# The taps of a state-space convolution: tables of powers and quarter-width products in place of 16 sine tables

## The chip, the cores and the metric

One core of one Trainium2 chip runs the program. The metric is the device time of one execution in microseconds (us), lower is better. The core's engines run side by side and wait for one another only through semaphores: TensorE (PE, with its weight loads as PEld), VectorE (DVE), ScalarE (ACT), GpSimd (POOL) and SyncE (SP), which issues the DMAs.

## The reference

The input x has 4 sequences of 1024 positions and 256 channels. Three residual steps are applied; the inputs of each are layer-normalized.

```
x = x + 0.5 * ffn(layernorm(x))
x = x + s4(layernorm(x))
x = x + 0.5 * ffn(layernorm(x))

ffn(x): h = silu(x w1' * w1_s) * (x w2' * w2_s)       # 256 -> 1024, ternary weights
        h = gelu(h h1' * h1_s); h = gelu(h h2' * h2_s)  # 1024 -> 1024, twice
        return h w3' * w3_s                             # 1024 -> 256
s4(x):  dt = exp(log_dt); A = -exp(log_A_real) + 1j * A_imag; dtA = A * dt   # 32 states per channel
        C = (C_real + 1j * C_imag) * (exp(dtA) - 1) / A
        K[d, t] = 2 * Re(sum_n C[d, n] * exp(dtA[d, n] * t))   # t = 0 .. 1023, the taps
        y = causal convolution of x with K along the positions (by FFT)
        return gelu(y) @ W' + b
```

The change touches only how the taps K are computed: 256 channels x 32 states x 1024 positions of complex exponentials, summed over the states.

## The kernel before

The 4096 rows are cut into tiles of 512. `ALL` = 16 tiles T = 0 to 15 go through the feed-forward net: T = 0 to 7 for the first ffn, T = 8 to 15 for the second. A tile has 24 steps k. Steps 0 to 7 are layer one: TensorE makes two products, VectorE gates them (`gate`), ScalarE and VectorE split the result into a high and a low part, since every product with activations is done for both (`hid_a_hi` and `hid_a_lo`, `hid_b_hi` and `hid_b_lo`). Steps 8 to 15 are the second layer and 16 to 23 the third, one `hidden` each: 16 matmuls 128x512 on TensorE, Gelu on ScalarE (L546), then `split` on VectorE (a CAST, L1167, and a subtraction, L1169). TensorE needs ScalarE's result of step k - 4 before it begins step k, because four PSUM banks go round, and ScalarE needs the split of step k - 3, because `act_o` has three slots. At k = 16 the inputs are the splits of steps 8 to 15, at `layer_three` (L1306) those of 16 to 23: there TensorE depends on the newest splits at once.

All order is written out by hand. Each engine runs through the same T and k in its own block of code, and the other work hangs on certain (T, k):

- `prepare` (VectorE, ScalarE, in T = 0 and 1) makes dt, decay and the angles from the parameters. A table of 8 block factors per channel and state is made by GpSimd (`angles8`, `powers8`, in T = 0 and 1).
- The taps. State and real or imaginary part lie on the 128 partitions, a pair of channels at each of 128 indices i, and a block of 128 positions on a table's columns. In 16 pieces c of `CH` = 8 indices each, placed by `turned_at` at every other k of T = 1 to 3, GpSimd makes the phases (`phase`, L473) and seven doublings of the decay (`doubles`, L482), VectorE reduces the phases to one turn (`turn_steps`, L844 to L848), ScalarE takes the sine (`sines`, L588), VectorE multiplies by the decay (`table_step`, L853), and TensorE multiplies (`tap_step`, L1313): 8 float32 matmuls with the 128-column table as weights and 16 columns (`kp`) that stream.
- The sums end in PSUM banks 4 to 7, are copied to `kt` in T = 3, and from T = 4 on are mirrored (`mirror_taps`), folded and transformed. T = 4 to 12 also carry the spectral convolution, one batch in two tiles.
- The layer norms (`norm_begin` L811 to L819, `norm_end` L824) sit on VectorE at the steps of `norm1_at` and `norm2_at`.

What `prepare` and `turn_steps` do on VectorE stands in its queue between two splits, so it delays every split behind it.

## Time and profile before

| | us |
|---|---|
| median of 3 runs | 1529.27 |
| lowest and highest | 1526.87, 1532.13 |
| the profiled execution | 1530.53 |
| its span, first to last instruction | 1528.7 |
| TensorE busy in the span | 1476.5 |
| VectorE, ScalarE, GpSimd busy | 1046.0, 521.9, 209.5 |
| mean granted TensorE clock | 0.988 of full |

A tile's time is read between two ends of its last product's scaling on VectorE (L1221). The span is the profiler's; the execution's own time is 1.8 us longer. In rows of the trace a number in square brackets is the idle time of that engine just before the instruction, with what ended it.

### The profile page before, as it was taken

How to read it: one execution, taken by the hardware profiler on the slowest of the kernel's cores; microseconds unless marked ns; L12 is line 12 of the kernel's file. 1: busy time of each engine (PE TensorE's matmuls, PEld its weight loads, DVE VectorE, ACT ScalarE, POOL GpSimd, SP SyncE). 2: the span in 40 equal slices, each digit the busy share in tenths (PEclk: the TensorE clock that was granted, in tenths of full speed). 3: DMA queues.
4: the chain of work that ended last, by engine and by line, in shares of the span. 5: the costliest groups of instructions: out<-in, count | busy, mean ns of one | idle time of the engine just before them, and what ended most of it. 6: DMA issues, size and time to landing. Idle time of an engine off the chain costs nothing.

```text
span 1528.7 us, 17472 instructions
## 1 busy us (share of the span) xinstructions
PE 1476.5 (97%) x6910; PEld 1192.3 (78%) x6910; DVE 1046.0 (68%) x1731; ACT 521.9 (34%) x743; POOL 209.5 (14%) x205
## 2 busy tenths in 40 slices
PE   7988979989999999999999999999999999999998
PEld 3767867777787778878778787787888878888886
DVE  7787576967857878785787848777587865343432
ACT  4623235445542332422323232232322324142321
POOL 0033553744600000001000010000000010000000
PEclk9999989999999999999999999999999999999999
DMA  8000000000001322103121031121221212000000
GB/s 347 15 0 28 28 14 15 28 15 14 28 15 39 116 91 83 43 25 124 42 83 56 13 123 56 55 70 39 68 69 42 69 38 69 0 15 28 29 1 15
DMA packets 52116, 78.27 MB, mean 51 GB/s; under 512 B 2752, under 2 KB 44736, under 8 KB 50624
## 3 DMA queue, kind: packets, MB, share of 16 engines
q1 hardware_dynamic: 52032, 77.12, 14.9%
q8 instruction: 56, 0.92, 0.2%
q14 instruction: 28, 0.23, 0.0%
HBM read 56.14 MB, written 20.97 MB: 50 GB/s over the span
## 4 chain that ended last, share of the span: by engine, by line
PE 81%; DVE 8%; issue 7%; ACT 3%; POOL 1%; DMA 0%; POOLq 0%; DVEq 0%; ACTq 0%
PE ps L1244 64%; PE ps L1306 7%; PE ps L1343 3%; PE ps L1396 2%; PE ps L1313 2%; DVE hid_a_lo L1169 1%; ACT L588 1%; DVE table L853 1%; ACT ph L588 1%; DVE hid_a_hi L1167 1%; DVE table L846 1%; PE ps L1235 1%; PE ps L1337 1%; PE ps L1338 1%; PE ps L1386 0%
## 5 line engine op out<-in xcount | busy, mean ns | idle before, releaser
L546 ACT ACTIVATE act_o<-ps,scales 128x512 f32<-128x512 f32 x384 | 263.8, 688 | 936.1 <-PE ps L1244 930.0
L1244 PE MATMUL ps<-hid_b_hi,h 128*128 128x512 f32 x1024 | 406.9, 397 | 4.9 <-DVE hid_b_lo L1169 4.7
L1244 PE MATMUL ps<-hid_b_lo,h 128*128 128x512 f32 x1024 | 403.3, 394 | 0.0
L1244 PE MATMUL ps<-hid_a_hi,h 128*128 128x512 f32 x992 | 395.8, 399 | 1.2 <-DVE hid_a_lo L1160 0.8
L1244 PE MATMUL ps<-hid_a_lo,h 128*128 128x512 f32 x992 | 390.8, 394 | 0.0
L1244 PEld LDWEIGHTS ps<-hid_b_hi,h 128*128 128x128 f32 x1024 | 193.6, 189 | 50.2 <-DVE hid_b_lo L1169 7.0
L1244 PEld LDWEIGHTS ps<-hid_b_lo,h 128*128 128x128 f32 x1024 | 193.5, 189 | 43.3 <-issue 1.2
L1244 PEld LDWEIGHTS ps<-hid_a_hi,h 128*128 128x128 f32 x992 | 187.6, 189 | 48.7 <-DVE hid_a_lo L1160 3.7
L1244 PEld LDWEIGHTS ps<-hid_a_lo,h 128*128 128x128 f32 x992 | 187.7, 189 | 42.1 <-issue 2.2
L1244 PE MATMUL ps<-hid_b_hi,w 128*128 128x512 f32 x480 | 190.0, 396 | 2.4 <-DVE gz L1221 2.1
L1244 PE MATMUL ps<-hid_b_lo,w 128*128 128x512 f32 x480 | 188.7, 393 | 0.0
L421 POOL TENSOR_TENSOR rstd<-vare,expo 128x4 f32<-128x4 f32 x24 | 27.9, 1163 | 920.1 <-DVE vare L819 920.1
L1167 DVE CAST hid_a_hi<-act_o 128x512 fp32r<-128x512 f32 x128 | 61.8, 483 | 129.3 <-ACT act_o L546 128.8
L1167 DVE CAST hid_b_hi<-act_o 128x512 fp32r<-128x512 f32 x128 | 55.4, 433 | 137.9 <-ACT act_o L546 137.6
L1306 PE MATMUL ps<-w,hid_a_hi 128*128 128x256 f32 x512 | 127.6, 293 | 15.2 <-DVE hid_a_lo L1169 9.6
L1155 DVE SCALAR_TENSOR_TENSOR gz<-ps,scales,act_o 128x512 f32<-128x512 f32 x128 | 96.0, 750 | 65.7 <-ACT act_o L546 64.0
L1306 PE MATMUL ps<-w,hid_a_lo 128*128 128x256 f32 x512 | 123.6, 285 | 0.0
L1244 PEld LDWEIGHTS ps<-hid_b_hi,w 128*128 128x128 f32 x480 | 90.1, 188 | 33.4 <-DVE gz L1155 8.1
L1306 PEld LDWEIGHTS ps<-w,hid_a_hi 128*128 128x128 f32 x512 | 100.9, 197 | 18.8 <-DVE hid_a_lo L1169 10.5
L1244 PEld LDWEIGHTS ps<-hid_b_lo,w 128*128 128x128 f32 x480 | 90.3, 188 | 16.1 <-issue 0.2
L1169 DVE TENSOR_TENSOR hid_a_lo<-act_o,hid_a_hi 128x512 fp32r<-128x512 f32 x128 | 99.3, 776 | 4.4
L1306 PEld LDWEIGHTS ps<-w,hid_a_lo 128*128 128x128 f32 x512 | 100.9, 197 | 1.1 <-issue 1.0
(228 smaller groups left out, 1597.6 us busy)
## 6 DMA issues: line engine op xcount, KB each, us to landing
ks<-k_d SPq DMA_DIRECT2D x32, 512.0 KB, 3.8
raws<-in_weights SPq DMA_DIRECT2D x11, 1024.0 KB, 15.6
gz<-in_x SPq DMA_DIRECT2D x8, 512.0 KB, 3.8
xin<-in_x SPq DMA_DIRECT2D x8, 512.0 KB, 3.9
x_d<-xin SPq DMA_DIRECT2D x8, 512.0 KB, 2.9
z_d<-xin SPq DMA_DIRECT2D x8, 512.0 KB, 2.9
k_d<-ks SPq DMA_DIRECT2D x8, 512.0 KB, 2.6
zb<-z_d SPq DMA_DIRECT2D x8, 512.0 KB, 5.4
```

The lines of the kernel that those rows point to most:

```text
L421: G.tensor_tensor(rstd[:, :], vare[:, :], expo[:, :], ALU.pow).then_inc(s_rstd, 1)
L546: A(act_o[:, k % ACT_SLOTS], bank(source), func, scale=scale).then_inc(s_act, 1)
L588: A(ph[:, c % 2], ph[:, c % 2], ACT.Sin, scale=TWO_PI_DOWN).then_inc(s_sin, 1)
L846: V.tensor_scalar(r_, r_, MAGIC, col(C_PH), ALU.subtract, ALU.subtract).then_inc(s_rnd, 1)
L1155: V.scalar_tensor_tensor(gated[:, m % 2], bank(2 * (m % 2) + 1), scales[:, 1, m:m + 1], act_o[:, m % ACT_SLOTS], ALU.mult, ALU.mult).then_ ...
L1167: V.tensor_copy(hi[:, k % KH], source).then_inc(s_hi, 1)
L1169: V.tensor_tensor(lo[:, k % KH], source, hi[:, k % KH].bitcast(F32), ALU.subtract).then_inc(s_split, 1)
L1244: last = MM(o, weight[:, k, cols].bitcast(dt), part[:, k].bitcast(dt), start=(k == 0 and i == 0), stop=(k == n - 1 and i == len(act_) - 1))
L1306: last = MM(o, part[:, k, j * P:(j + 1) * P].bitcast(dt), w3[:, k].bitcast(dt), start=(k == 0 and i == 0), stop=(k == KH - 1 and i == 1))
L1313: last = MM(ps[:, 4 + i // 32, (i % 32) * 2 * A8:(i % 32 + 1) * 2 * A8], table[:, c % 2, i % CH, :], kp[:, i, 0:2 * A8], start=True, stop= ...
L1343: last = MM(bank(o), tables[:, table_], flat(x), start=True, stop=True)
L1396: last = MM(o, ga[:, k, u * P:(u + 1) * P], wt[:, k], start=(k == 0), stop=(k == KD - 1))
```

## The change

Before, a tap's position is t = 128 a + q, with 8 blocks a and a table of 128 positions q that needs a sine for each entry. Now it is t = 32 a + q with 32 positions q and 32 blocks a, both tables are products of small tables of powers, and no sine is left in the loop over pieces. `prepare` now makes ten seeds: the complex exponential at 1, 2, 4, ... 512 positions (`ea` the sizes, `sn` and `cs` the sine and cosine), with two sine instructions of 1280 columns in T = 1 (`sines`) and the reciprocals in parts of 128 columns. From the seeds VectorE and ScalarE multiply up two small tables per channel, `v` (8 powers) and `u` (4 powers), each once for the positions and once for the blocks; 4 x 8 = 32 (`SPAN`) entries come from each pair of tables. For each of 8 pieces of 16 indices, `make_factors` on VectorE forms the 32-column tables `tab` and `gr` (six operations 128x512), ScalarE writes `gr` masked by channel half into the 64 columns of `gm`, and `multiply_taps` on TensorE does 16 float32 matmuls with 32 weight columns and 64 streaming columns, each with its result in one quarter of the 128 partitions of PSUM. `MADE`, `MASKED` and `MULTIPLIED` say at which (T, k) each stands. GpSimd's work on the taps goes away but for four memsets. Since the sums now lie by quarters, ScalarE copies them out at T = 3, k = 17 into `wb`, and SyncE turns them by a DMA to memory and four back into `zb` (`turn_taps`). Several norms move by one to three steps, and the rest of the coefficient arithmetic moves from T = 0 into T = 1. Nothing from T = 4, k = 8 on is altered.

```diff
+SEEDS = 10
 EXPS = SEEDS // 2
-KPAR = 2 * A8 + 1 + DBL
+NV, NU = 8, 4
+PIECE = 16
+PIECES = P // PIECE
+SPAN = NU * NV
...
-def turned_at(T):
-    return {1: {20: 0, 22: 1}, 2: {8 + 2 * i: 2 + i for i in range(8)},
-            3: {8 + 2 * i: 10 + i for i in range(6)}}.get(T, {})
+MADE = {(2, 17): 0, (2, 19): 1, (2, 21): 2, (3, 8): 3, (3, 9): 4, (3, 10): 5, (3, 11): 6, (3, 14): 7}
+MASKED = {(2, 18): 0, (2, 20): 1, (2, 22): 2, (3, 9): 3, (3, 10): 4, (3, 11): 5, (3, 12): 6, (3, 15): 7}
+MULTIPLIED = {(2, 20): 0, (2, 22): 1, (3, 8): 2, (3, 11): 3, (3, 12): 4, (3, 13): 5, (3, 14): 6, (3, 17): 7}
...
+            def turn_taps():
+                sp.wait_ge(s_kev, 1)
+                sp.dma_start(t_d, wb[:, :, :].rearrange("p u d -> p (u d)")).then_inc(s_kd, 16)
+                sp.wait_ge(s_kd, 16)
+                by_block = t_d.rearrange("(g t) (b f) -> b t g f", g=4, b=4)
+                for b in range(4):
+                    home = zb[32 * b:32 * b + 32].rearrange("t u d -> t (u d)").rearrange("t (g f) -> t g f", g=4)
+                    sp.dma_start(home, by_block[b]).then_inc(s_kt, 16)
...
-            def phase(c):
-                if c >= 2:
-                    pool.wait_ge(s_table, c - 1)
-                G.tensor_tensor(ph[:, c % 2], kp[:, c * CH:(c + 1) * CH, 2 * A8:2 * A8 + 1].to_broadcast([P, CH, P]),
-                                taps[:, :].unsqueeze(1).to_broadcast([P, CH, P]), ALU.mult).then_inc(s_phase, 1)
-            def doubles(c):
-                if c:
-                    pool.wait_ge(s_table, c)
-                for k in range(DBL):
-                    n = 1 << k
-                    seed = kp[:, c * CH:(c + 1) * CH, 2 * A8 + 1 + k:2 * A8 + 2 + k].to_broadcast([P, CH, n])
-                    G.tensor_tensor(dec[:, :, n:2 * n], dec[:, :, 0:n], seed, ALU.mult).then_inc(s_dbl, 1)
-                    pool.wait_ge(s_dbl, c * DBL + k + 1)
...
+            pool.wait_ge(s_seed, 1)
+            for powers, value in ((vre, 1.0), (vim, 0.0), (ure, 1.0), (uim, 0.0)):
+                last = G.memset(powers[:, :, :, 0:1], value)
+            last.then_inc(s_units, 1)
...
-            def sines8(h):
-                act.wait_ge(s_arg8, h + 1)
-                for i in (0, 1):
-                    A(tap8[:, i], tap8[:, i], ACT.Sin, scale=TWO_PI_DOWN).then_inc(s_sin8, 1)
+            def sines():
+                act.wait_ge(s_arg, 3)
+                A(sn[:, :], cs[:, :], ACT.Sin, scale=TWO_PI_DOWN).then_inc(s_fun, 1)
+                act.wait_ge(s_fun, 4)
+                A(cs[:, :], cs[:, :], ACT.Sin, scale=PI_DOWN).then_inc(s_fun, 1)
+            def copy_seeds(homes, v, k):
+                for home, seeds in zip(homes, (cs, sn)):
+                    A(home[:, :, :, v], seeds[:, k:k + EXPS + 1:EXPS], ACT.Copy).then_inc(s_copied, 1)
...
+                    act.wait_ge(s_arg, 4)
+                    A(et[:, :], er[:, :], ACT.Tanh, scale=0.5)
                     A(tmp[:, 5], tmp[:, 9], ACT.Tanh, scale=0.5).then_inc(s_fun, 1)
-                    for i in (2, 3, 4):
-                        A(tmp[:, 4 + i], tmp[:, i], ACT.Sin, scale=TWO_PI_DOWN).then_inc(s_fun, 1)
-                if T == 1 and k == 2:
-                    sines8(0)
-                if T == 1 and k == 15:
-                    sines8(1)
...
+                    copy_seeds((vre, vim), 4, 2)
+                    copy_seeds((ure, uim), 1, 3)
+                    copy_seeds((ure, uim), 2, 4)
+                if T == 2 and k == 10:
+                    act.wait_ge(s_tabled, 1)
+                    act.wait_ge(s_units, 1)
+                    act.wait_ge(s_copied, 10)
+                    A(xt[:, 0], uim[:, 0], ACT.Copy, scale=small[:, C_NRE:C_NRE + 1])
+                    A(xt[:, 1], ure[:, 0], ACT.Copy, scale=small[:, C_RE:C_RE + 1]).then_inc(s_turned, 1)
+                if (T, k) in MASKED:
+                    n = MASKED[T, k]
+                    act.wait_ge(s_factor, n + 1)
+                    if n:
+                        act.wait_ge(s_tap, n)
+                    for j in range(2):
+                        last = A(gm[:, :, j], gr[:, :, :], ACT.Copy, scale=small[:, C_H + j:C_H + j + 1])
+                    last.then_inc(s_masked, 1)
...
-                if T == 3 and k == PER_U - 2:
-                    act.wait_ge(s_tap, SUBS)
-                    for i in (0, 2):
-                        last = A(zb[:, 2 * i:2 * i + 4].rearrange("p u d -> p (u d)"), bank(4 + i, 2), ACT.Copy)
-                    last.then_inc(s_kt, 1)
+                if T == 3 and k == 17:
+                    act.wait_ge(s_tap, PIECES)
+                    sums = ps[:, 4:8, :].rearrange("p n c -> p (n c)").rearrange("p (f a b) -> p b f a", a=A8, b=4)
+                    homes = wb[:, :, :].rearrange("p u d -> p (u d)").rearrange("p (b f a) -> p b f a", b=4, a=A8)
+                    for b in range(4):
+                        last = A(homes[:, b], sums[:, b], ACT.Copy)
+                    last.then_inc(s_kev, 1)
                 if T == 4:
...
                 if T == 0 and k == 11:
                     dve.wait_ge(s_fun, 1)
+                    step(V.tensor_scalar(er[:, 0:2], et[:, 0:2], -1.0, 1.0, ALU.mult, ALU.add))
+                    step(V.reciprocal(er[:, 0:2], er[:, 0:2]))
+                if T == 0 and k == 12:
                     step(exp_finish(tmp[:, 0:2], 2))
-                    step(V.scalar_tensor_tensor(decay, ar, -1.0, dt_, ALU.mult, ALU.mult))
+                    V.scalar_tensor_tensor(decay, ar, -1.0, dt_, ALU.mult, ALU.mult).then_inc(s_arg, 1)
                     step(V.tensor_tensor(tmp[:, 10], ai, dt_, ALU.mult))
-                    V.tensor_scalar(turns, tmp[:, 10], INV_TWO_PI, None, ALU.mult)
-                    for i in range(EXPS):
-                        last = V.tensor_scalar(ea[:, i], decay, float(4 ** i), None, ALU.mult)
+                    step(V.tensor_scalar(cs[:, 0], tmp[:, 10], INV_TWO_PI, None, ALU.mult))
+                if T == 0 and k == 15:
+                    for first, n in ((1, 1), (2, 2), (4, 1), (5, 5)):
+                        step(V.tensor_scalar(cs[:, first:first + n], cs[:, 0:n], float(2 ** first), None, ALU.mult))
+                    step(V.tensor_scalar(sn[:, :], cs[:, :], MAGIC, -MAGIC, ALU.add, ALU.add))
+                if T == 0 and k == 16:
+                    V.tensor_tensor(cs[:, :], cs[:, :], sn[:, :], ALU.subtract).then_inc(s_arg, 1)
+                    dve.wait_ge(s_fun, 2)
+                    exp_reduce(ea[:, 0:EXPS], EXPS, 0)
+                if T == 0 and k == 17:
+                    exp_reduce(ea[:, 0:EXPS], EXPS, 1)
+                if T == 0 and k == 18:
+                    exp_reduce(ea[:, 0:EXPS], EXPS, 2).then_inc(s_arg, 1)
+                if T == 0 and k == 19:
+                    V.tensor_tensor(a2, ar, ar, ALU.mult)
+                    step(V.tensor_tensor(q1, ai, ai, ALU.mult))
+                    step(V.tensor_tensor(q2, a2, q1, ALU.add))
+                    step(V.reciprocal(a2, q2))
+                if T == 0 and k == 20:
+                    dve.wait_ge(s_fun, 3)
+                    step(V.tensor_scalar(er[:, :], et[:, :], -1.0, 1.0, ALU.mult, ALU.add))
+                if T == 0 and k in (20, 21):
+                    for i in range(EXPS)[0 if k == 20 else 2:2 if k == 20 else EXPS]:
+                        last = V.reciprocal(er[:, i], er[:, i])
                     step(last)
...
+                if T == 1 and k == 8:
                     step(exp_finish(ea[:, 0:EXPS], EXPS))
                     step(V.tensor_tensor(ea[:, EXPS:], ea[:, 0:EXPS], ea[:, 0:EXPS], ALU.mult))
...
+                if T == 1 and k == 9:
+                    dve.wait_ge(s_fun, 5)
+                    step(V.scalar_tensor_tensor(cs[:, :], cs[:, :], -2.0, cs[:, :], ALU.mult, ALU.mult))
+                    step(V.tensor_copy(versed, cs[:, 0]))
+                    step(V.tensor_scalar(cs[:, :], cs[:, :], 1.0, None, ALU.add))
...
+                if T == 1 and k in (17, 18):
+                    seeds = (sn, cs)[k - 17][:, :].rearrange("p (i h) q -> p i h q", h=2)
+                    sizes = ea[:, :].rearrange("p (h i) q -> p i h q", h=2)
+                    last = V.tensor_tensor(seeds, seeds, sizes, ALU.mult)
+                    if k == 17:
+                        step(last)
+                    else:
+                        last.then_inc(s_seed, 1)
...
+                if (T, k) in ((1, 21), (2, 8)):
+                    part = 2 - T
+                    if T == 1:
+                        dve.wait_ge(s_copied, 4)
+                    x = vre[:, :, :, 1:4], vim[:, :, :, 1:4]
+                    y = [h.unsqueeze(3).to_broadcast([P, 2, P, 3]) for h in power(2)]
+                    last = product((vre[:, :, :, 5:8], vim[:, :, :, 5:8]), x, y, ct[:, :, :, :], T - 1)
+                    if T == 1:
+                        step(last)
+                    else:
+                        last.then_inc(s_tabled, 1)
...
+            def make_factors(n):
+                q = slice(n * PIECE, (n + 1) * PIECE)
+                wide = [P, PIECE, NU, NV]
+                for s_, out_ in ((0, tab[:, n % 2]), (1, gr[:, :, :])):
+                    if s_ == 0 and n >= 2:
+                        dve.wait_ge(s_tap, n - 1)
+                    if s_ == 1 and n:
+                        dve.wait_ge(s_masked, n)
+                    out_ = out_.rearrange("p q (u v) -> p q u v", v=NV)
+                    extra = pt[:, :, :].rearrange("p q (u v) -> p q u v", v=NV)
+                    for to, u, v in ((out_, (uim, ure)[s_], vre), (extra, (ure, uim)[s_], vim)):
+                        last = V.tensor_tensor(to, u[:, s_, q].unsqueeze(3).to_broadcast(wide),
+                                                v[:, s_, q].unsqueeze(2).to_broadcast(wide), ALU.mult)
+                    step(last)
+                    last = V.tensor_tensor(out_, out_, extra, ALU.add)
+                    if s_:
+                        last.then_inc(s_factor, 1)
                     else:
                         step(last)
...
-            def turn_steps(c):
-                p_, r_ = ph[:, c % 2], table[:, c % 2]
-                dve.wait_ge(s_phase, c + 1)
-                if c >= 2:
-                    dve.wait_ge(s_tap, c - 1)
-                V.tensor_scalar(r_, p_, col(C_PH), MAGIC, ALU.add, ALU.add).then_inc(s_rnd, 1)
-                dve.wait_ge(s_rnd, 2 * c + 1)
-                V.tensor_scalar(r_, r_, MAGIC, col(C_PH), ALU.subtract, ALU.subtract).then_inc(s_rnd, 1)
-                dve.wait_ge(s_rnd, 2 * c + 2)
-                V.tensor_tensor(p_, p_, r_, ALU.subtract).then_inc(s_red, 1)
-            def table_step(c):
-                dve.wait_ge(s_sin, c + 1)
-                dve.wait_ge(s_dbl, (c + 1) * DBL)
-                V.tensor_tensor(table[:, c % 2], ph[:, c % 2], dec[:, :, :], ALU.mult).then_inc(s_table, 1)
...
-            def tap_step(c):
-                pe.wait_ge(s_table, c + 1)
-                for i in range(c * CH, (c + 1) * CH):
-                    last = MM(ps[:, 4 + i // 32, (i % 32) * 2 * A8:(i % 32 + 1) * 2 * A8], table[:, c % 2, i % CH, :],
-                              kp[:, i, 0:2 * A8], start=True, stop=True)
+            def multiply_taps(n):
+                pe.wait_ge(s_masked, n + 1)
+                for i in range(PIECE):
+                    r, g = divmod(n * PIECE + i, 4)
+                    width = 2 * SPAN
+                    at = r % 8 * width
+                    last = MM(ps[SPAN * g:SPAN * (g + 1), 4 + r // 8, at:at + width], tab[:, n % 2, i],
+                              gm[:, i].rearrange("p j a -> p (j a)"), start=True, stop=True)
                 last.then_inc(s_tap, 1)
...
-                pe.wait_ge(s_kt, 1)
+                pe.wait_ge(s_kt, 16 * 4)
```

TensorE in the third layer of a tile, T = 3. Before, a tap step stands in front of every other `hidden` (33 rows apart, eight in T = 2 and eight in T = 3):

```order
1229 L1244 MATMUL ps<-hid_a_hi,h_51 128x512
1230 L1244 MATMUL ps<-hid_a_lo,h_51 128x512
1231 L1313 MATMUL ps<-kp,table 128x16 x8
1232 L1244 MATMUL ps<-hid_a_hi,h_51 128x512
1233 L1244 MATMUL ps<-hid_a_lo,h_51 128x512
```

and now (two of these pieces in T = 2, six in T = 3, four of them at successive k):

```order
1206 L1249 MATMUL ps<-hid_a_hi,h_51 128x512
1207 L1249 MATMUL ps<-hid_a_lo,h_51 128x512
1208 L1321 MATMUL ps<-gm,tab 32x64 x16
1209 L1249 MATMUL ps<-hid_a_hi,h_51 128x512
1210 L1249 MATMUL ps<-hid_a_lo,h_51 128x512
```

The stop has twice as many matmuls, a quarter of the weight columns and four times the streaming columns, and there are half as many stops.

VectorE in T = 0 at k = 11 and 12, before; `ek`, `er`, `et` are the exponential's parts, `ea` the sizes:

```order
50 L726 TENSOR_SCALAR er<-et 128x256
51 L727 RECIPROCAL er<-er 128x256
52 L728 SCALAR_TENSOR_TENSOR er<-et,er 128x256
53 L729 TENSOR_TENSOR tmp<-er,ek 128x256
54 L749 SCALAR_TENSOR_TENSOR tmp<-tmp 128x128
55 L750 TENSOR_TENSOR tmp<-par,tmp 128x128
56 L751 TENSOR_SCALAR kp<-tmp 128x128
57 L753 TENSOR_SCALAR ea<-tmp 128x128 x5
58 L1167 CAST hid_b_hi<-act_o 128x512
59 L1169 TENSOR_TENSOR hid_b_lo<-act_o,hid_b_hi 128x512
60 L716 TENSOR_SCALAR ek<-ea 128x640
```

and now:

```order
50 L711 TENSOR_SCALAR er<-et 128x256
51 L712 RECIPROCAL er<-er 128x256
52 L1173 CAST hid_b_hi<-act_o 128x512
53 L1175 TENSOR_TENSOR hid_b_lo<-act_o,hid_b_hi 128x512
54 L675 SCALAR_TENSOR_TENSOR er<-et,er 128x256
55 L676 TENSOR_TENSOR tmp<-er,ek 128x256
56 L715 SCALAR_TENSOR_TENSOR tmp<-tmp 128x128
57 L716 TENSOR_TENSOR tmp<-par,tmp 128x128
58 L717 TENSOR_SCALAR cs<-tmp 128x128
59 L1173 CAST hid_b_hi<-act_o 128x512
```

The work of k = 11 is spread over two steps, and the seven operations on 640 columns that began at row 60 follow only behind k = 15.

## Rows read from the trace of the kernel before

In the windows a row is the stretch and its length in us, the busy us (and instructions) of PE, PEld, DVE, ACT and POOL, the granted TensorE clock as a share of full speed, the DMA share and GB/s.

**Rows 1.** Windows, one row for each of T = 0 to 3, then T = 14.

```profile
0.00:127.36 127.36, 107.05 (x409) 75.64 (x410) 96.74 (x167) 51.07 (x59) 16.29 (x19) 0.96 0.28 109
127.36:223.52 96.16, 87.09 (x394) 71.65 (x393) 64.57 (x94) 32.73 (x46) 54.53 (x47) 0.93 0.07 22
223.52:333.78 110.26, 101.60 (x522) 84.17 (x521) 86.16 (x111) 53.69 (x61) 59.15 (x66) 0.97 0.06 20
333.78:438.90 105.12, 99.80 (x519) 82.28 (x518) 73.76 (x105) 51.88 (x60) 42.67 (x49) 0.98 0.07 21
...
1359.55:1441.33 81.78, 81.78 (x394) 67.77 (x393) 35.61 (x66) 24.66 (x37) 1.01 (x1) 1.00 0.06 20
```

**Rows 2.** Waits of TensorE, 0 to 534.2 us: total, times, longest.

```profile
PE ps L1313 <- DVE table L853: 10.5, 14, 0.8
PE ps L1306 <- DVE hid_a_lo L1169: 9.6, 4, 3.5
...
PE ps L1306 <- ACT act_o L546: 4.9, 2, 4.3
PE ps L1244 <- DVE hid_b_lo L1169: 4.7, 3, 2.3
```

**Rows 3.** Waits of TensorE in T = 0 alone, 0 to 127.36 us.

```profile
PE ps L1306 <- DVE hid_a_lo L1169: 3.3, 2, 3.0
```

**Rows 4.** Timeline of TensorE around one tap step in T = 2.

```profile
245.58 0.39 PE L1244 MATMUL ps<-hid_a_hi,h 128*128 128x512 f32 x1
245.81 0.40 PE L1244 MATMUL ps<-hid_a_lo,h 128*128 128x512 f32 x1
246.95 1.96 PE L1313 MATMUL ps<-kp,table 128*128 128x16 f32 x16 [0.74 <-DVE table L853]
248.76 0.48 PE L1244 MATMUL ps<-hid_a_hi,h 128*128 128x512 f32 x1
```

**Rows 5.** Windows: two stretches of low granted clock, T = 2 and T = 1.

```profile
249.65:253.06 3.41, 3.41 (x10) 2.65 (x9) 2.51 (x4) 0.00 (x0) 3.02 (x6) 0.51 0.00 0
...
205.20:218.85 13.65, 8.35 (x37) 8.05 (x38) 9.61 (x9) 4.12 (x5) 8.74 (x10) 0.50 0.00 0
```

**Rows 6.** Timeline of T = 0, VectorE and TensorE, 66 to 84 us.

```profile
66.73 1.75 DVE L727 RECIPROCAL er<-er 128x256 f32<-128x256 f32 x1
...
71.03 0.43 DVE L1167 CAST hid_b_hi<-act_o 128x512 fp32r<-128x512 f32 x1
...
76.33 0.42 DVE L1167 CAST hid_b_hi<-act_o 128x512 fp32r<-128x512 f32 x1
...
82.40 0.69 DVE L1169 TENSOR_TENSOR hid_b_lo<-act_o,hid_b_hi 128x512 fp32r<-128x512 f32 x1
...
83.15 0.79 PE L1244 MATMUL ps<-hid_b_hi,h 128*128 128x512 f32 x1 [1.89 <-DVE hid_b_lo L1169]
```

**Rows 7.** Timeline of the end of T = 1.

```profile
196.60 3.98 POOL L473 TENSOR_TENSOR ph<-kp,taps 128x1024 f32<-128x1024 f32 x2
196.66 2.14 DVE L1167 CAST hid_a_hi<-act_o 128x512 fp32r<-128x512 f32 x1
...
203.87 1.06 ACT L588 ACTIVATE ph<-ph 128x1024 f32<-128x1024 f32 x1 [3.70 <-DVE ph L848]
...
206.98 0.58 PE L1306 MATMUL ps<-w,hid_a_hi 128*128 128x256 f32 x1 [4.29 <-ACT act_o L546]
```

**Rows 8.** Groups by line: operations nearest to the new ones; last numbers: busy, mean ns.

```profile
L1313 PE MATMUL ps<-kp,table 128*128 128x16 f32 x256 | 31.3, 264 | 10.5 <-DVE table L853 10.5
...
L588 ACT ACT_TABLE_LOAD x16 | 20.5, 1283 | 0.3
...
L874 DVE TENSOR_TENSOR wb<-ps,zb 128x256 f32<-128x256 f32 x4 | 2.4, 594 | 0.0
```

**Rows 9.** The one-column matmul's line: weight loads, ns min/median/max.

```profile
L1448 PEld LDWEIGHTS ps<-single x2: 79/80/81, 54.9 to 54.9; 128*1 128x1 f32 x2
```

**Rows 10.** Timeline: eight float32 passes of 512 columns in T = 10.

```profile
1037.35 3.60 PE L1343 MATMUL ps<-fb,tables 128*128 128x512 f32 x8
```

314 lines of the change are left out of this document (121 added, 193 removed).

## The prediction

> **What bounds the kernel now.** I first split the span by tiles. A tile without taps or spectral work, T = 14, takes 81.78 us, and TensorE is busy for all of it. T = 1, 2 and 3 take 96.16, 110.26 and 105.12 us, and T = 0 takes 127.36 [rows 1]. So TensorE sets the end everywhere, and T = 1 to 3 hold 14.4 + 28.5 + 23.3 = 66.2 us above the plain tile. Next the waits of TensorE in this stretch: 9.6 and 4.9 us stand before layer three and 4.7 us before the third layer at k = 16, together 19.2 us in few, long waits, and 10.5 us stand before tap steps in 14 short ones [rows 2]. Then one tap step in the timeline: the last `hidden` matmul starts at 245.81, the next could start 0.23 us later, and starts at 248.76. The step costs 2.72 us: 0.74 us of waiting for the table, 16 passes at 0.112 us (1.96 us less the tail of the last), and small rests [rows 4]. Last the clock: 249.65 to 253.06 is granted 0.5, the lower level of 1.2 GHz against 2.4, just after such a step; in T = 1, 205.20 to 218.85 is low, around two long waits before layer three [rows 5]. The granted clock times the length gives 5.1 us lost in T = 0, and 6.7, 3.3 and 2.1 in T = 1 to 3 [rows 1]; in T = 1 TensorE stood still for 5.3 of the 13.65 low us [rows 5], so only 4.2 us count there, 14.7 in all.
>
> These three causes close the account: T = 1 to 3 have 11.1 us of the long waits (19.2 less 4.7 and 3.3 in T = 0 [rows 2, 3]), 16 x 2.72 = 43.5 us of tap steps and 9.6 us of clock, 64.2 of the 66.2 us.
>
> **The change, part by part.**
>
> *T = 0, VectorE's queue.* At k = 11 and 12 `prepare` holds it from the reciprocal at 66.73 to the CAST at 71.03, and again from that split's end to 76.33: with 1.1 us for the split in between, 4.6 us (a scalar operation of 0.3 is ahead of the reciprocal) and 4.2 us. Behind them the norm and three splits queue up, the last ends at 83.09, and TensorE stops for it, 1.89 us at that place [rows 6]. Now k = 11 is 0.3 + 1.8 us and k = 12 about 1.7 us. 8.8 - 3.8 = 5.0 us less lie before split 15, more than the 4.7 us of waits, which go. The seven operations on 640 columns come after k = 15 in three parts, each with its split under 3.7 us, and a `hidden` is 16 x 0.23 = 3.67 us [rows 4]: TensorE covers them. Behind k = 22 and 23, where the coefficient arithmetic stood, nothing is left, so T = 0's 3.3 us before layer three [rows 3] go too.
>
> *T = 1, ScalarE and VectorE.* TensorE's 4.29 us wait goes back to ScalarE, which stood 3.70 us for VectorE's reduced phases, and VectorE was late since a CAST that takes 0.43 us elsewhere took 2.14 us beside GpSimd's phases [rows 6, 7]. Phases and sines are gone. In their place the sines of 1280 columns, 2 x 1.3 + 1.28 us for the table [rows 7, 8], stand on ScalarE ahead of step 8. That makes split 8 about 4 us late. VectorE's new work in k = 8 to 14 is 2.6, 2.7, 2.4 us, by about 1.05 us for 1000 elements of a product, then two norms of 3.4 (76.33 to 83.09 is one norm and three splits of 1.1 [rows 6]); with seven splits of 1.1 us that is 22.2 us against 25.7 us of TensorE, so the 4 us shrink to about half a microsecond where split 15 is needed. This is the thinnest cover: if it fails, up to 4 us of wait return. From k = 15 to 21 the parts are 1.4 to 3.0 us, and ScalarE's ten seed copies are 0.4 us each, all inside a step.
>
> *Layer boundaries together:* 19.2 us go, and I leave 1.0 us for the new ones: -18.2.
>
> *The pieces on VectorE and ScalarE.* A piece is six operations of two inputs on 128x512, as the 0.69 us of L1169 [rows 6], 4.2 us, with a split 5.3 us. Four stand at successive k = 8 to 11 of T = 3. TensorE's step there is 3.67 us and a piece of matmuls, t; with t of 1.7 us or more VectorE keeps up. The masks are two ScalarE operations of 512 columns, some 0.6 us each by 1.06 for 1024 [rows 7]; each is placed a step or more ahead of its matmuls, in T = 2 with a margin of about nothing for the first. The piece at k = 14 ends close to the need at k = 16. What is late next there is split 15, 0.2 to 0.5 us, in the 1.0 us above. VectorE's table work was five operations on 1024 columns for each of 16 steps.
>
> *The matmuls.* 8 stops of 32 passes replace 16 of 16. Lower bound of a pass: by streaming alone. Eight passes of 512 columns take 3.60 us, less a tail 0.43 us each, 0.84 ns a column [rows 10], so 64 columns take 0.054 us. Upper bound of a pipelined pass: as before, 0.112 us [rows 4], which a 16-column stream cannot set, so the weight load or the issue does. A load of one column takes 0.080 us [rows 9], a load of T = 14, nearly all of 128 columns, 0.172 us (67.77 us by 393 [rows 1]); 32 columns lie nearer the first. I take 0.083, the middle, since the issue rate is unknown. t = 32 x 0.083 + 0.15 to enter = 2.8 us, 8 t = 22.4 instead of 43.5: -21.1. With the bounds t is 1.8 or 3.7 and the term -29 or -14.
>
> The Trainium skill (TensorE: Matmul & The Clock Gate, LDWEIGHTS) has the load go by its columns alone, which would let streaming set the pass: an estimate of 7 us less than my sum. By that section the one-column load must be the shorter one, and the trace agrees, 0.080 against 0.172 us [rows 1, 9]; no row has 32 columns.
>
> *Clock.* 14.7 us are lost now. The long waits that stood beside three of the low stretches go; eight stops instead of sixteen remain. Of the sixteen one in T = 2 had a low stretch behind it [rows 5], 1.7 us, and the 2.1 us of T = 3, which has no long wait, are about one more [rows 1, 2]. I keep 4 us: -10.7.
>
> *Tap layout.* ScalarE copies out at k = 17 (four of 512 columns, 2.4 us) and the round trip is five DMAs. TensorE asks at T = 4, k = 0, six steps, transposes and layer three later, over 29 us. Hidden; with no cover it would cost its own time, some 10 us. The mirror matmuls and folds keep count and size, 0; if the new stride doubled the streaming of the mirror's eight passes of 256 columns, 0.215 us each by 0.84 ns a column [rows 10], it would be +1.7.
>
> Sum: -18.2 - 21.1 - 10.7 = -50.0. The profiled execution took 1530.53 us, 1.3 over the median of the three runs, so against that median **1529.3 - 50 = 1479 us**.
>
> **The rivals.**
>
> *Same pace, more low clock (20 of 100).* A pass stays at 0.112 us: t = 3.7, +7 us. A stop is then longer than the old one, and each may be followed by a low stretch as after 248.76 [rows 4, 5]: 8 x 1.7 = 13.6 instead of 4, +10. 1486 to 1496. For it: the 16-column pass shows that something else than streaming sets the pace. Against: the stream is four times longer, and a load has a quarter of the columns.
>
> *Quarters at the same time (10 of 100).* Four successive matmuls use four different quarters of the output. If they overlap, a stop is streaming by four, 0.5 us, 8 t = 4 to 5 us instead of 22. Then VectorE sets the pace at four successive pieces, 5.3 us against 4.2, and gives 4 us back: 1465. No row here has two matmuls at once. The Trainium skill says it can be so (TensorEngine Tiling (Array Packing), Key Properties: tiles work independently, weight loads and matmuls in parallel).
>
> *VectorE becomes the bound (10 of 100).* The one product here that reads with large steps, L874, takes 0.594 us for 256 elements [rows 8], where a plain product of 512 takes 0.69 [rows 6]. If repeated and stepped operands make a product of 512 elements 1.05 us, a piece is 6.3 and a step 7.4 us against 6.5: four pieces lose 4 us, k = 14 loses 2 to 3, T = 1's tables the rest of their cover: 1487. Against: the innermost operand of each product is dense or repeats.
>
> *The other side: drained quarters (5 of 100).* If each pass must wait until the one before has left the array, it costs a load and a full matmul, 0.08 to 0.19 + 0.264 us [rows 8, 9], t = 11 to 14.6, 8 t = 88 to 117: 1545 to 1573. It decides from t = 2.8 + 50/8 = 9.0 us, 0.28 us a pass. Milder, a drain only where a stop begins and ends costs 0.26 us each by the same row, 4 us in all, inside the range. The Trainium skill (TensorEngine Tiling (Array Packing), Key Properties) has such a rule: a change of tiling mode drains TensorE, a change of the tile alone does not.
>
> **How the numbers follow.** 55 of 100 for the sum as worked out, with 1468 to 1489 as its own range (t from 1.8 to 3.2, clock 0 to 8 us, waits 0 to 5). The rivals have 20, 10, 10 and 5. The range takes in all but the drained quarters and the outer ends: 1464 to 1500. A difference of 0.3%, 4.6 us, is about what a measurement of this kernel can tell from none. Faster: 93, within: 2, slower: 5.
>
> **What would show it.** Right: T = 0 near 114 us, T = 1 near 83, T = 2 near 88, T = 3 near 100; no wait over 1 us before k = 16 or layer three; starts of the new passes 0.055 to 0.112 us apart; no GpSimd beside VectorE in T = 1 to 3. Wrong: passes over 0.2 us apart; ScalarE late at step 8 of T = 1 and a wait at its k = 16; TensorE waiting for ScalarE's masks in T = 3; low clock behind most of the eight stops; the mirror matmuls of T = 4 waiting for a DMA.

## The result, and the profile after

| | before | after |
|---|---|---|
| median, us | 1528.90 (4 runs) | 1461.55 (4 runs) |
| lowest and highest | 1526.87, 1532.13 | 1461.34, 1463.29 |
| the profiled execution, its span | 1530.53, 1528.7 | 1463.29, 1461.0 |
| TensorE busy | 1476.5 | 1437.8 |
| VectorE, ScalarE, GpSimd busy | 1046.0, 521.9, 209.5 | 986.4, 476.6, 48.1 |
| mean granted clock | 0.988 | 0.998 |

The ratio is 0.956, 95% interval 0.9542 to 0.9579: 67 us less, where 50 were forecast. 1461.55 lies 2.5 us below the range. The same windows as in [rows 1]:

```profile
0.00:115.01 115.01, 102.36 (x409) 72.35 (x410) 82.06 (x131) 48.71 (x59) 2.47 (x8) 1.00 0.31 120
115.01:196.78 81.77, 81.77 (x394) 67.76 (x393) 63.37 (x127) 32.21 (x49) 4.42 (x6) 1.00 0.08 26
196.78:280.46 83.68, 83.61 (x458) 68.75 (x457) 57.99 (x109) 29.93 (x45) 2.01 (x2) 1.00 0.08 26
280.46:369.49 89.03, 87.33 (x583) 70.11 (x582) 57.73 (x110) 32.97 (x51) 2.12 (x2) 1.00 0.16 48
```

T = 0 to 3 are 12.4, 14.4, 26.6 and 16.1 us shorter, 69.4 in all. T = 1 is now a plain tile: TensorE is busy for all of it, while VectorE has 63 us of work beside it. The granted clock is full in all four. The one new loss is behind them, at the start of T = 5, where the clock is low for 3.41 us (1.7 us lost):

```profile
465.80:469.21 3.41, 3.41 (x10) 2.63 (x9) 1.33 (x3) 0.76 (x2) 0.00 (x0) 0.50 0.84 263
```

The waits of TensorE over the first 534 us, where [rows 2] had 29.7 us at four places. The 2.1 us stand at the start of T = 5, which in the kernel before lay just behind this window:

```profile
PE ps L1249 <- DVE gz L1226: 2.1, 1, 2.1
PE ps L1321 <- ACT gm L534: 1.6, 3, 0.5
...
PE ps L1249 <- DVE hid_b_lo L1175: 0.3, 1, 0.3
```

L1249 is `hidden`, L1321 the taps' matmul, L534 the mask, L1175 the split's subtraction. Nothing before layer three is left in T = 0 to 3. One stop for the taps in the timeline, answering [rows 4]:

```profile
332.82 0.40 PE L1249 MATMUL ps<-hid_b_lo,h 128*128 128x512 f32 x1
333.15 0.65 PE L1321 MATMUL ps<-gm,tab 128*32 128x64 f32 x32
333.73 0.51 PE L1249 MATMUL ps<-hid_b_hi,h 128*128 128x512 f32 x1
```

From the `hidden` matmul before to the one behind it are 0.91 us, 0.23 of which are that matmul's own: the stop costs 0.68 us, for 32 passes. The price of each of the eight is 0.67 to 0.82 us with no wait or one under 0.1 us, and 1.26 to 1.28 where the mask is late, 7.4 us in all. The sixteen of before, priced in the same way, cost 41.6 us and not the 43.5 of the prediction: 2.72 us holds for the fourteen with a wait, but the first stop of T = 2 and the first of T = 3 had none and cost 1.70 us each:

```profile
236.69 0.39 PE L1244 MATMUL ps<-hid_b_lo,w 128*128 128x512 f32 x1
236.92 1.85 PE L1313 MATMUL ps<-kp,table 128*128 128x16 f32 x16
238.62 0.48 PE L1244 MATMUL ps<-hid_a_hi,h 128*128 128x512 f32 x1
```

The 32 starts within the first new stop, in ns after one another:

```
7 7 6 60 7 7 6 36 7 6 7 36 7 6 ...   last start 435 ns after the first
```

Four passes start within 20 ns, and then there is a gap. The profile does not name the quarters; that the four go into four different ones is inferred from the run one_quarter below, where passes into the same quarter never start less than 55 ns apart. The groups by line:

```profile
L534 ACT ACTIVATE gm<-gr,small 128x512 f32<-128x512 f32 x16 | 10.7, 716 | 15.3 <-DVE gr L832 15.3
...
L829 DVE TENSOR_TENSOR tab<-uim,vre 128x512 f32<-128x512 f32 x8 | 5.5, 685 | 0.0
...
L1321 PE MATMUL ps<-gm,tab 128*32 128x64 f32 x256 | 5.2, 222 | 1.6 <-ACT gm L534 1.6
L1321 PEld LDWEIGHTS ps<-gm,tab 128*32 128x32 f32 x256 | 3.9, 109 | 4.9 <-ACT gm L534 4.1 <-issue 0.7
...
L1329 PE MATMUL ps<-zb,flip 128*128 128x256 f32 x8 | 3.6, 608 | 0.0
```

The matmul's row has 222 ns for one from start to end and the load's 109, so a pass does not finish in 7 ns: several are under way at once (the profile models a matmul's end, but the starts and the price of the stop do not hang on it). In both rows x256 counts passes, two for each float32 matmul.

### The profile page after: what moved, and what is told of

It is laid out like the page before. It is cut to its first block, busy times and chain, and to the rows that moved or that the text cites. A ratio compares the mean times of both kernels' runs of the same rounds, so it can differ in the third digit from the quotient of the medians.

```text
span 1461.0 us, 17259 instructions
## 1 busy us (share of the span) xinstructions
PE 1437.8 (98%) x6910; PEld 1159.7 (79%) x6910; DVE 986.4 (68%) x1729; ACT 476.6 (33%) x721; POOL 48.1 (3%) x42
## 3 DMA queue, kind: packets, MB, share of 16 engines
q1 hardware_dynamic: 52464, 79.15, 16.1%
## 4 chain that ended last, share of the span: by engine, by line
PE 92%; DVE 6%; ACT 1%; issue 1%; DMA 0%; POOL 0%; DVEq 0%; ACTq 0%; POOLq 0%
PE ps L1249 76%; PE ps L1311 8%; PE ps L1344 3%; PE ps L1397 2%; PE ps L1240 1%; DVE hid_b_lo L1175 1%; PE ps L1338 1%; PE ps L1339 1%; DVE pt L829 1%; PE ps L1387 0%; DVE hid_b_hi L1173 0%; ACT act_o L476 0%; DVE low L1140 0%; DVE tab L832 0%; DVE gr L832 0%
## 5 line engine op out<-in xcount | busy, mean ns | idle before, releaser
L1249 PE MATMUL ps<-hid_b_hi,h 128*128 128x512 f32 x1024 | 404.4, 395 | 0.5 <-DVE hid_b_lo L1175 0.3
L1249 PE MATMUL ps<-hid_b_lo,h 128*128 128x512 f32 x1024 | 401.6, 392 | 0.0
L1249 PE MATMUL ps<-hid_a_hi,h 128*128 128x512 f32 x992 | 393.1, 396 | 0.2
L1249 PE MATMUL ps<-hid_a_lo,h 128*128 128x512 f32 x992 | 388.7, 392 | 0.0
L1249 PEld LDWEIGHTS ps<-hid_b_hi,h 128*128 128x128 f32 x1024 | 192.5, 188 | 44.8 <-DVE hid_b_lo L1175 1.4
L1249 PEld LDWEIGHTS ps<-hid_b_lo,h 128*128 128x128 f32 x1024 | 192.5, 188 | 43.1 <-issue 1.2
L1249 PEld LDWEIGHTS ps<-hid_a_hi,h 128*128 128x128 f32 x992 | 186.3, 188 | 47.5 <-DVE hid_a_lo L1166 2.8
L1249 PEld LDWEIGHTS ps<-hid_a_lo,h 128*128 128x128 f32 x992 | 186.4, 188 | 41.4 <-issue 2.2
L1249 PE MATMUL ps<-hid_b_hi,w 128*128 128x512 f32 x480 | 190.3, 396 | 2.1 <-DVE gz L1226 2.1
L1249 PE MATMUL ps<-hid_b_lo,w 128*128 128x512 f32 x480 | 189.6, 395 | 0.0
L1173 DVE CAST hid_a_hi<-act_o 128x512 fp32r<-128x512 f32 x128 | 56.7, 443 | 135.4 <-ACT act_o L476 134.7
L1311 PE MATMUL ps<-w,hid_a_hi 128*128 128x256 f32 x512 | 123.0, 286 | 0.8 <-ACT act_o L476 0.8
L1311 PE MATMUL ps<-w,hid_a_lo 128*128 128x256 f32 x512 | 119.8, 279 | 0.0
L1249 PEld LDWEIGHTS ps<-hid_b_hi,w 128*128 128x128 f32 x480 | 90.6, 189 | 32.5 <-DVE gz L1161 7.8
L1249 PEld LDWEIGHTS ps<-hid_b_lo,w 128*128 128x128 f32 x480 | 90.9, 189 | 16.3 <-issue 0.2
L1311 PEld LDWEIGHTS ps<-w,hid_a_hi 128*128 128x128 f32 x512 | 96.6, 189 | 3.3 <-ACT act_o L476 1.2
L1311 PEld LDWEIGHTS ps<-w,hid_a_lo 128*128 128x128 f32 x512 | 96.6, 189 | 1.1 <-issue 1.0
L1175 DVE TENSOR_TENSOR hid_a_lo<-act_o,hid_a_hi 128x512 fp32r<-128x512 f32 x128 | 88.6, 693 | 4.4
L1175 DVE TENSOR_TENSOR hid_b_lo<-act_o,hid_b_hi 128x512 fp32r<-128x512 f32 x128 | 88.6, 692 | 4.4
```

The costliest lines, as they stand in the source:

```text
L1173: V.tensor_copy(hi[:, k % KH], source).then_inc(s_hi, 1)
L1175: V.tensor_tensor(lo[:, k % KH], source, hi[:, k % KH].bitcast(F32), ALU.subtract).then_inc(s_split, 1)
L1249: last = MM(o, weight[:, k, cols].bitcast(dt), part[:, k].bitcast(dt), start=(k == 0 and i == 0), stop=(k == n - 1 and i == len(act_) - 1))
L1311: last = MM(o, part[:, k, j * P:(j + 1) * P].bitcast(dt), w3[:, k].bitcast(dt), start=(k == 0 and i == 0), stop=(k == KH - 1 and i == 1))
```

## The experiments

**One quarter.** All 16 products of a piece go to the same quarter of PSUM's partitions (the sums lie elsewhere, so the taps are not those of the reference; the work is the same).

```diff
-                    last = MM(ps[SPAN * g:SPAN * (g + 1), 4 + r // 8, at:at + width], tab[:, n % 2, i],
-                              gm[:, i].rearrange("p j a -> p (j a)"), start=True, stop=True)
+                    g, slot = n // 2, n % 2 * PIECE + i
+                    last = MM(ps[SPAN * g:SPAN * (g + 1), 4 + slot // 8, slot % 8 * width:(slot % 8 + 1) * width],
+                              tab[:, n % 2, i], gm[:, i].rearrange("p j a -> p (j a)"), start=True, stop=True)
```

> All 16 products of a piece go to one quarter of the partitions (pieces 0 and 1 to the first, 2 and 3 to the second, and so on), same weight loads, same streams, same count; the sums land in the wrong places, so the taps are wrong. Theory A: neighbouring products overlap because they use different quarters. Then the 32 passes of a piece follow one another at 0.054 (streaming) to 0.112 us (the old pass), a piece costs 1.9 to 3.7 us in place of 0.67 to 0.82, eight of them +9 to +24 us: 1470 to 1486 us. Rival B: a pass of 32 weight columns and 64 streaming columns is short by itself, whatever the quarter: starts stay 7 to 60 ns apart and the time stays at 1461.5.

**Two quarters** in turn within a piece (the taps again misplaced).

```diff
+                    g, slot = n // 4 * 2 + i % 2, n % 4 * (PIECE // 2) + i // 2
```

> The products of a piece alternate between two quarters; the sums land in the wrong places. Theory A: two passes at a time, a piece costs about half of the one-quarter piece, 1.0 to 1.9 us. Rival B: no change, 0.7 us a piece.

**Grouped.** The changed kernel's own 16 products, with those of the same quarter behind one another.

```diff
-                for i in range(PIECE):
+                for i in [4 * b + a for a in range(4) for b in range(PIECE // 4)]:
```

> The same 16 products with the same places as in the changed kernel, in another order: four for the first quarter, then four for the second, and so on. Theory A with overlap only between neighbours of different quarters: overlap at 3 of 15 borders alone, a piece costs 1.5 to 3 us. Theory A with a queue for each quarter that is filled ahead: as in the changed kernel, 0.7 us. Rival B: 0.7 us.

**Full width.** Four positions' tables together as 128 weight columns, all quarters at once, 64 columns streaming (the taps are not those of the reference).

```diff
-                    last = MM(ps[SPAN * g:SPAN * (g + 1), 4 + r // 8, at:at + width], tab[:, n % 2, i],
+                    four = tab[:, n % 2, i // 4 * 4:i // 4 * 4 + 4].rearrange("p q a -> p (q a)")
+                    last = MM(ps[:, 4 + r // 8, at:at + width], four,
```

> Each product has 128 weight columns (the tables of four indices side by side) and the same 64 streaming columns, and fills all 128 partitions; three quarters of each result are overwritten or useless, so the taps are wrong. If 128 weight columns set the pass as before, starts are 0.112 us apart, a piece costs 3.7 us and the eight cost +24 us less the 1.6 us of mask waits: 1483 to 1486. If streaming sets it, 0.054 us, 1.9 us a piece, about 1470. If the count of passes alone matters (rival B), 1461.5. Also: whether stops of 3.7 us are followed by a low granted clock, which would add up to 1.7 us each (the prediction's second rival, up to 1499).

**Narrow stream.** As full width, but 16 columns stream.

```diff
-                              gm[:, i].rearrange("p j a -> p (j a)"), start=True, stop=True)
+                              gm[:, i, 0, 0:16], start=True, stop=True)
```

> The changed kernel, but each of the 16 products of a piece takes four positions' tables as weights (all 128 columns, all 128 partitions of the result) and streams only 16 columns, as the tap products of the kernel before did; the taps are then not those of the reference. If the load of 128 weight columns sets the pace, a pass is 0.112 us apart as in the kernel before and as with 64 streaming columns, a piece costs 3.4 to 3.6 us, and the whole is 1484 to 1487 us. If streaming counted beside the load, 16 columns would go faster than the 64 of full_width: under 0.10 us a pass and below 1482. On the clock: if stops with a thin stream bring low clock by themselves, low stretches follow the pieces of T = 2 and 3 here; if they came from the waits that stood before them, none does.

**Quarter narrow and four narrow.** One quarter, and the changed kernel, with 16 streaming columns.

> one_quarter with 16 streaming columns in place of 64 (the taps are not those of the reference; the first piece also has four products 128x512 ahead of its own, so that no sum is unset, some 3.5 us once). It settles what the 0.056 us of a pass in one quarter is. If streaming sets it, 0.84 ns by 16 columns would be 0.013 us, and a pass falls to whatever the load of 32 weight columns needs, 0.03 us by a quarter of 0.112: first to last start of a piece about 0.9 us and a piece 1.2. Rival: the load and the entry of the next pass in the same quarter set it, then passes stay 0.056 us apart and a piece costs 2.0 us. On the clock: if a stream of 16 columns is what brings the clock down, a low stretch may follow here too, though the stop is shorter than in narrow_stream.

> The changed kernel with 16 streaming columns in place of 64, the four quarters in turn as in the changed kernel (the same parts of the computation are altered as in quarter_narrow). Four neighbours start 7 ns apart and a group takes 56 ns. If streaming sets the group, 16 columns make it 30 ns or less and a piece falls from 0.70 to 0.5 us; if four loads of 32 columns, 14 ns each, set it, a piece stays at 0.67 to 0.70 us. The time is then 1461 to 1465 us (3.5 us of it for the first piece's extra products).

**Twice.** The changed kernel with the loop over a piece's products run two times.

```diff
-                for i in range(PIECE):
+                for i in list(range(PIECE)) * 2:
```

> The changed kernel with each piece's 16 products issued twice, the second time with the same operands into the same places, so 64 passes in a stop. It separates what a pass costs from what it costs to enter and leave a stop. If the passes cost what their starts show (32 in 0.435 us), a piece of 0.70 to 0.82 us becomes 1.15 to 1.3, eight give +3.0 to 3.8 us: 1464.5 to 1467. Rival: the starts are only issue and the array works longer behind them, or most of a piece is entry: then the second half costs 0.7 us or more each (+5.6, 1469), or under 0.2 us (+1.5, 1463 to 1465).

What the eight kernels gave beside the changed one, measured as above (steady distance of starts within a piece; a piece without a wait; all eight pieces, with waits, and without the extra products of the two that have them):

| kernel | weight columns, streaming | distance of starts, ns | first to last, us | a piece, us | eight, us | span, us |
|---|---|---|---|---|---|---|
| full_width | 128, 64 | 112 | 3.41 | 3.49 | 28.5 | 1482.2 |
| narrow_stream | 128, 16 | 112 | 3.38 | 3.49 | 30.0 | 1490.9 |
| one_quarter | 32, 64 | 56 | 1.76 | 1.99 | 16.2 | 1466.6 |
| quarter_narrow | 32, 16 | 32 | 1.00 | 1.21 | 10.1 | 1465.5 |
| grouped | 32, 64 | 56, and 6, 50, 30, 26, 30, 26, 30 across borders | 1.18 | 1.42 | 11.5 | 1462.4 |
| two_quarters | 32, 64 | 7 and 49: 56 a pair | 0.87 | 1.11 | 9.5 | 1461.9 |
| changed kernel | 32, 64 | 7, 7, 7, 36: 56 a group | 0.44 | 0.68 | 7.4 | 1461.0 |
| four_narrow | 32, 16 | 7, 7, 7, 12: 32 a group | 0.26 | 0.47 | 6.3 | 1462.6 |
| twice | 32, 64, 64 passes | as the changed kernel | 0.88 | 1.12 | 9.6 | 1463.1 |

Two ran four times: one_quarter 1470.99 (ratio to before 0.9608, 0.9575 to 0.9642), full_width 1485.24 (0.9698, 0.9665 to 0.9731). The other six ran once each (two_quarters 1464.06, grouped 1464.64, narrow_stream 1493.01, twice 1465.34, quarter_narrow 1467.59, four_narrow 1464.76), so what follows rests on their traces, not on these times. Four of the stops as timelines show them, one_quarter, full_width, narrow_stream and four_narrow:

```profile
340.00 1.98 PE L1322 MATMUL ps<-gm,tab 128*32 128x64 f32 x32
```

```profile
328.27 0.39 PE L1249 MATMUL ps<-hid_a_lo,h 128*128 128x512 f32 x1
328.50 3.68 PE L1322 MATMUL ps<-gm,tab 128*128 128x64 f32 x32
331.99 0.48 PE L1249 MATMUL ps<-hid_a_hi,h 128*128 128x512 f32 x1
```

```profile
326.03 3.64 PE L1322 MATMUL ps<-gm,tab 128*128 128x16 f32 x32
```

```profile
336.06 0.45 PE L1324 MATMUL ps<-gm,tab 128*32 128x16 f32 x32
```

A piece in one quarter costs 2.0 us and in four 0.68, with the same operands and counts. That shows that the quarters overlap; a pace set by the issue of instructions would have been the same in both. The prices of a piece in quarter_narrow, four_narrow and twice came as the first theory of each had them; their spans hold the first piece's extra products (the first two) and no low clock at T = 5 (twice). All eight pieces of twice cost 2.2 us more than the changed kernel's, not the 3.0 to 3.8 expected, because at three of them the added passes only fill the time in which TensorE waited for a mask. narrow_stream has the pace expected and 6 us more than the time expected, for which see the clock below.

What follows, step by step. *The load:* with 128 weight columns a pass is 0.112 us for 16 and for 64 streaming columns, so the load set it in the kernel before too. With 32 it is 0.056 us in one quarter; 16 streaming columns bring it to 0.032. So at 64 columns streaming sets the pass (0.84 ns by 64 is 0.054, my lower bound's argument), and the floor below it is 0.032, little over a quarter of 0.112. That this floor is the load is argued from that proportion. *The quarters:* two in turn take the 56 ns for a pair, four for a group of four. The time is that of one quarter's stream, shared. The products' order matters: grouped has the changed kernel's own products and needs 1.42 us in place of 0.68. Neither theory had that number. Overlap of the two neighbours at each of the three borders alone would save about 3 x 0.05 us of one_quarter's 1.76 from first to last start, but grouped needs 1.18. Eight passes in a row go to each quarter, yet already behind the fifth the next starts after 6 ns, which one_quarter never shows; so passes of the next quarter start before the last ones of the quarter before. They reach a few passes ahead, and not far enough to undo the order. *Entry:* doubling the passes adds 0.45 us to a piece, 1.12 less 0.67, and 32 starts took 0.435; the other 0.24 us are paid once per stop (0.20 with 16 streaming columns). full_width's stops, which use all four quarters at once, have none of it: their first pass starts 0.23 us behind the `hidden` matmul, as any matmul there does, and the next `hidden` one 0.08 us after the last pass, against 0.33 and 0.15 us around the changed kernel's. As a check, the span less the eight pieces, and less 1.7 us where the clock is low at T = 5 (full_width, the changed kernel), is 1452.0, 1450.4, 1450.9, 1452.4 and 1451.9 us for full_width, one_quarter, grouped, two_quarters and the changed kernel. Nothing else of size moves with the pace.

The Trainium skill (TensorE: Matmul & The Clock Gate, LDWEIGHTS) has the load go by its columns alone; 0.112 and 0.032 us agree to within 15% of proportion. The Trainium skill (TensorEngine Tiling (Array Packing), Key Properties) has tiles work independently, which the 7 ns starts show; the drain that it asks for at a change of mode would lie within the 0.24 us per stop, which full_width's stops lack and no run here splits further.

**The clock under a thin stream.** If waits are the cause of low clock, none of these kernels should have a low stretch in T = 2 and 3. full_width has none in T = 2 and 3; narrow_stream, with stops as long and no waits before them, has five, 23.9 us, each during or behind one of five of its eight stops:

```profile
269.40:272.81 3.41, 3.41 (x10) 2.65 (x9) 1.48 (x3) 0.00 (x0) 0.00 (x0) 0.50 0.00 0
303.60:310.43 6.83, 6.83 (x21) 5.67 (x21) 0.24 (x1) 1.02 (x2) 0.00 (x0) 0.50 0.25 79
337.70:341.11 3.41, 3.41 (x10) 2.63 (x9) 0.00 (x0) 0.65 (x2) 0.67 (x1) 0.50 0.00 0
344.50:351.33 6.83, 6.83 (x23) 5.86 (x23) 0.97 (x4) 0.00 (x0) 0.00 (x0) 0.50 0.44 147
365.00:368.41 3.41, 3.41 (x9) 2.67 (x8) 0.00 (x0) 0.00 (x0) 0.00 (x0) 0.50 0.00 0
```

T = 2 and 3 take 205.5 us here against 193.1 in full_width: half of 23.9, as the lower of the two levels (1.2 of 2.4 GHz) says. So stops of 3.5 us with 128 weight columns and 16 streaming ones can bring the clock down without a wait, and stops of the same length with 64 columns did not, each in one trace. quarter_narrow and four_narrow, thin but short (1.21 and 0.47 us), have none in T = 2 and 3. The kernel before streamed 16 columns too, but for 1.7 us and mostly behind a wait of 0.74, and had three low stretches in T = 2 and 3; how much of them was the thin stream and how much the waits, no run shows.

**Spread alone.** The kernel before with one edit in T = 0: the large block on VectorE moved from k = 12 to 15, and the reduction of the angles from 15 to 16.

```diff
-                if T == 0 and k == 12:
+                if T == 0 and k == 15:
                     exp_reduce(ea[:, 0:EXPS], EXPS).then_inc(s_arg, 1)
-                if T == 0 and k == 15:
+                if T == 0 and k == 16:
```

> The kernel before, with one edit alone: in T = 0 VectorE's seven operations on 640 columns (exp_reduce of the sizes) stand at k = 15 instead of k = 12, and the reduction of the angles at k = 16 instead of k = 15. My step says that the block ahead of split 12 is what made split 15 late: with it gone TensorE's waits at k = 16 of T = 0 (4.7 us) go, the low clock behind them gives 1 to 3 us back, and the wait before layer three (3.3 us) stays or grows by up to 2 us, since the work is moved towards it. That is 1521 to 1525 us against 1529. Rival: T = 0 is late for another reason (the tables of parameters, ScalarE), then the waits only move from k = 16 to layer three and the time is 1527 to 1531. T = 1 to 3 keep 96, 110 and 105 us under both.

1529.36 us in 10 runs against 1531.18, ratio 0.999 (0.9973 to 1.0008): no change that can be told. TensorE's waits in T = 0, where before the two were 4.7 and 3.3:

```profile
PE ps L1306 <- DVE hid_a_lo L1169: 6.3, 2, 3.6
...
PE ps L1244 <- DVE hid_b_lo L1169: 1.0, 1, 1.0
```

Most of the wait at k = 16 went, as my step says (-3.7), and came back before layer three (+3.0), more than the 2 I allowed. The rival has it: moving the block alone pays nothing that the times can tell, and at most 4 us by their interval. In the profiled execution T = 0 is 2.9 us shorter (124.48), and 1.8 of them are time that TensorE no longer loses to the low clock; a single execution can't settle a gain of that size. T = 0 lost its low clock and its waits in the changed kernel, where the coefficient arithmetic of k = 22 and 23 is gone too; that this makes the difference is my reading, and no run here has it alone.

**Late turn.** The changed kernel with the last mirror product and fold moved from the end of T = 4 into T = 5.

```diff
+                    if T == 5 and m == 5:
+                        finish_taps(7)
...
-                    for i in (6, 7):
-                        finish_taps(i)
+                    finish_taps(6)
...
+                if T == 5 and k == 4:
+                    turn(7)
...
-                    turn(7)
```

> The changed kernel with one edit: the last mirror product and its fold (unit 7 of the taps' layout) go from the end of T = 4 into T = 5, behind layer one's fifth step, so that VectorE has one fold less between the norm and the scaling that TensorE waits 2.1 us for at the start of T = 5. If that fold is what makes the scaling late, the wait falls from 2.1 to 0.8 us or less, and the low clock of 3.41 us behind it goes where it came: 1461.5 becomes 1459 to 1460.5. Rival: the wait is that of the row sums or of another chain into the scaling and stays at 2.1 us: 1461.5 within 0.5.

It gave 1459.23 us (1458.63 to 1464.02, 5 runs), with a ratio to before of 0.9532 (0.9509 to 0.9555). Since the changed kernel had not run on that chip, both ran again side by side.

> The changed kernel once more, unaltered, so that the next two stand beside it on one chip: 1461 to 1463.5 us, and a profile with the 2.1 us wait at the start of T = 5; the low clock of 3.41 us behind that wait comes in some executions and not in others (the two levels of its times, 1461.3 and 1463.3, are this far apart).

> The late turn of the last tap unit once more, beside the unaltered changed kernel. Its profile showed the wait at T = 5 split into 0.7 and 0.5 us in place of 2.1, so it should be 0.9 us faster than the changed kernel, and up to 1.7 more in executions in which the other has the low clock: 1458.5 to 1461. If the difference is under 0.5 us, what the tile T = 4 gained is given back in T = 5, which was 93.1 us in place of 92.1 to 93.9.

changed_again: 1463.61 median (1461.66 to 1465.2), late_turn_again: 1459.85 (1458.29 to 1463.72), 5 runs each; the means are 2.8 us apart, but the runs overlap. The wait of T = 5 is 2.1 us in the one, and in the other there are two short ones:

```profile
PE ps L1251 <- DVE gz L1164: 0.7, 1, 0.7
PE ps L1251 <- DVE gz L1228: 0.5, 1, 0.5
```

That is 0.9 us less, and T = 4 and 5 together take 188.25 and 187.22 us. The rest of the difference can't be assigned: it is no larger than what single executions differ by (below). My explanation of the two levels of times failed as well: the profiled execution of changed_again has no low stretch at T = 5 and took 1463.61.

**Masks on two engines.** The late turn, with the second mask on GpSimd.

```diff
-                    for j in range(2):
-                        last = A(gm[:, :, j], gr[:, :, :], ACT.Copy, scale=small[:, C_H + j:C_H + j + 1])
-                    last.then_inc(s_masked, 1)
+                    A(gm[:, :, 0], gr[:, :, :], ACT.Copy, scale=small[:, C_H:C_H + 1]).then_inc(s_masked, 1)
...
+                G.tensor_tensor(gm[:, :, 1], gr[:, :, :], half, ALU.mult).then_inc(s_masked, 1)
```

> The late turn, and the second of the two masks of each piece on GpSimd (a product with the channel-half column, 128x512) instead of ScalarE, so that both are written at the same time. If the two masks in a row are what TensorE waits 0.5 us for at three pieces, the masks are ready 0.3 to 0.5 us earlier (GpSimd's 1.0 us, half of L473's for 1024 columns, against 2 x 0.71) and the waits of 1.5 us fall to about 0.5: 1 us faster than the late turn. Rival: VectorE's casts and scalar operations beside a GpSimd product are slowed, as the 2.14 us CAST of rows 7 was, VectorE's pace in T = 3 is the bound anyway, and the waits stay or grow to 3 us: 0 to 2 us slower.

1465.42 us (1460.76 to 1465.48, 4 runs). The rival has the waits: the three grow from 1.6 to 3.6 us, and T = 3 takes 91.5 us where late_turn and late_turn_again have 88.7 and 89.0. The median is 5.6 us above late_turn_again's, more than the rival's 0 to 2; but the profiled execution is the fastest of the four, 1460.76, so no trace shows where the 5.6 come from. Waits, and two groups of 285 to 330 us:

```profile
PE ps L1333 <- POOL gm L446: 3.6, 3, 1.2
PE ps L1261 <- DVE hid_b_lo L1188: 0.9, 1, 0.9
```

```profile
L1188 DVE TENSOR_TENSOR hid_b_lo<-act_o,hid_b_hi 128x512 fp32r<-128x512 f32 x7 | 7.7, 1101 | 0.2
...
L446 POOL TENSOR_TENSOR gm<-gr,small 128x512 f32<-128x512 f32 x4 | 4.6, 1155 | 48.4 <-DVE gr L843 48.4
```

GpSimd's mask takes 1.16 us. The split's subtraction is 1.10 us in the mean in place of 0.69, and that mean mixes two lengths: the four that begin 0.29 us after a mask take 1.41 us each, the other three 0.69. The CASTs, which begin before the mask, stay at 0.42 us, so it is not the operations that the rival named which were slowed.

**GpSimd beside VectorE.** Idle products on GpSimd in T = 14 of the changed kernel.

```diff
+            def load(T):
+                for k in range(KH, PER_U, 2):
+                    pool.wait_ge(s_split, at_split(T, k))
...
+                    G.tensor_tensor(wb[:, 0:4], zb[:, 0:4], zb[:, 4:8], ALU.mult)
+                    G.tensor_tensor(wb[:, 4:8], zb[:, 0:4], zb[:, 4:8], ALU.mult).then_inc(s_idle, 1)
```

> The changed kernel with idle work on GpSimd in T = 14, a tile in which it has nothing else to do: two products of 128x1024 behind every other split of the second and third layer, 16 in all, of operands that nobody needs. My step on T = 1 blames GpSimd for VectorE's lateness. Then in T = 14 VectorE's CAST goes from 0.43 to as much as 2.1 us wherever it meets a product, its subtraction of 0.69 us much less or not at all, the split at the end of a layer is late, and T = 14 takes 82.5 to 85 us in place of 81.78. Rival: the long CAST of the kernel before came from something else (ScalarE, a DMA, the operands' places); then no operation of VectorE changes by over 0.1 us and T = 14 stays at 81.8 us.

T = 14 takes 95.30 us (one execution) in place of 81.7 to 82.0, far more than I expected. VectorE and GpSimd in its timeline:

```profile
1327.82 9.83 DVE L864 TENSOR_SCALAR gz<-gz,mv,rstd 128x256 f32<-128x256 f32 x4
...
1337.57 0.41 DVE L1183 CAST hid_b_hi<-act_o 128x512 fp32r<-128x512 f32 x1
1337.64 2.54 POOL L439 TENSOR_TENSOR wb<-zb 128x1024 f32<-128x1024 f32 x1
1338.01 2.71 DVE L1185 TENSOR_TENSOR hid_b_lo<-act_o,hid_b_hi 128x512 fp32r<-128x512 f32 x1
1340.14 2.80 POOL L440 TENSOR_TENSOR wb<-zb 128x1024 f32<-128x1024 f32 x1
1340.65 2.57 DVE L1183 CAST hid_b_hi<-act_o 128x512 fp32r<-128x512 f32 x1
...
1348.51 0.69 DVE L1185 TENSOR_TENSOR hid_a_lo<-act_o,hid_a_hi 128x512 fp32r<-128x512 f32 x1
1349.28 2.39 POOL L439 TENSOR_TENSOR wb<-zb 128x1024 f32<-128x1024 f32 x1 [1.09 <-DVE hid_a_lo L1185]
```

The four scalar operations of the norm take 9.83 us, against 1.39 in the changed kernel where GpSimd is idle:

```profile
76.29 1.39 DVE L854 TENSOR_SCALAR gz<-gz,mv,rstd 128x256 f32<-128x256 f32 x4 [0.18 <-POOL rstd L426]
```

A CAST of 0.43 us takes 2.57, as the one in [rows 7]. Each of these comes to about the length of one GpSimd product. Of the sixteen subtractions fourteen stay at 0.69 us and two take 2.7, which I had not expected either. They are no more immune than the CASTs: the two are the ones that began while a product was running, and the others ran before the first product, between two products, or began ahead of one. TensorE waits 10.15 us in the tile and has 10.24 us of low clock. So a GpSimd product alone can make VectorE's operations as long as they were in T = 1 of the kernel before; there it was GpSimd's phases that ran beside them.

## Why the prediction was wrong

The account of what bound the kernel held at nearly every step. The step that failed is the price of the new stops: 22.4 us were forecast and 7.4 measured, because passes into different quarters overlap, which the sum excluded. That carries most of the miss.

- **The matmuls, the step that failed.** I took 0.083 us a pass and t = 2.8 us a stop, with 1.8 as the lower bound "by streaming alone". Measured: 0.435 us for 32 starts and 0.24 to enter, t = 0.68, 7.4 us in all with the mask waits. The term is -34.2 us (41.6 less 7.4), not -21.1, and outside my own bounds of -29 and -14. Three errors lie in it. The middle between 0.054 and 0.112 was wrong: one quarter runs at 0.056, the lower end. The lower bound was none, since it let passes only follow one another. And the old stops were taken too dear, 16 x 2.72 = 43.5, though two of them had no wait; that gives 1.9 of the 15 us back. The rival "Quarters at the same time" is what happened; I gave it 10 in 100 because no row showed two matmuls at once, though no row spoke against it either. Its 1465 is 3.5 us over what came, near by errors that offset each other: its stops, 4 to 5 us, were 7.4, VectorE gave back 1.6 us, not 4, and clock and layer boundaries gave some 5 more than the sum had.
- **Layer boundaries, -18.2:** measured -20.0 (TensorE's idle in T = 0 to 3 falls from 43.4 to 14.4 us; less 10.5 and 1.6 that belong to the stops). The cover in T = 1 that I called the thinnest held: no wait at all. spread_alone shows that the move of k = 12 by itself mostly moved the wait: with the old queue behind it, 3.0 of the 3.7 us came back before layer three. Which of the other changes in T = 0 removed it was not tested, nor was T = 1 without GpSimd's phases; pool_load only shows that GpSimd's products can do what was seen there.
- **The clock, -10.7:** measured -13.7, half of the 27.5 us in which TensorE was busy at the lower level in T = 0 to 3 before; no low stretch remains there. I kept 4 us for the stops. In full_width's trace even stops of 3.5 us bring none in T = 2 and 3 where 64 columns stream, so of the rival "Same pace, more low clock" the pace was possible and the 10 us of clock would hardly have come. The reason I gave, long waits, need not be all of it: narrow_stream shows low clock without a wait.
- **The pieces on VectorE.** An operation takes 685 to 692 ns for 512 columns with repeated operands, the 0.69 I assumed, so the rival's 1.05 is out. With t below 1.7 VectorE does set the pace, as I wrote: the four successive stops start 5.05 us apart, where TensorE would need 3.67 + 0.68. It costs 3 waits of 0.5 us.
- **Tap layout and mirror, 0:** the mirror matmul takes 608 ns in both kernels. No wait for the round trip.
- **Behind T = 3:** the low clock at T = 5, +1.7, was not in my sum; the wait of 2.1 us before it was there before and had none.

The account: -20.0 - 34.2 - 13.7 = -67.9 of the -69.4 in T = 0 to 3. The other 1.5 us belong to no term here. With +1.7 behind T = 3 it is -67.7, the difference of the spans. Of the tiles forecast, T = 0 and 1 came within 2 us (114 and 83 forecast), and T = 2 and 3 fell short by 4 and 11 (88 and 100), where the stops are. Of the signs of being wrong one came, the waits for the masks in T = 3. Drained quarters are out.

## What to carry to other kernels

In these runs a small matmul's pass cost what goes by its weight columns or its stream, whichever was longer (128 and 64 or 16 columns: 112 ns; 32 and 64: 56; 32 and 16: 32), and passes into different quarters of the partitions shared that time. So order the products so that successive ones go to different quarters. A lower bound that treats operations as a queue is not a lower bound where the engine can overlap them; if nothing in the trace tells, that case deserves a large chance and its place in the range. A stop that mostly loads weights can also cost clock: streaming 64 columns instead of 16 left the pace of a 128-column pass as it was and took away 23.9 us at the lower level. Beside a GpSimd product of 2.4 us a VectorE CAST of 0.43 us took 2.57 us, so look for both when a split is late.

## What the runs showed that I had not expected

- With full granted clock in the records, the steady distance of `hidden` matmuls is 229 ns in most stretches and 233.3 in some: T = 14 of late_turn_again takes 83.07 us, the tile before it 82.00, with equal work.

```profile
1210.07:1292.07 82.00, 82.00 (x394) 67.99 (x393) 35.63 (x65) 24.69 (x37) 1.02 (x1) 1.00 0.06 20
1292.07:1375.14 83.07, 83.07 (x394) 68.28 (x393) 35.65 (x66) 24.69 (x37) 1.02 (x1) 1.00 0.06 20
```

  In changed_again it is T = 1, 83.06 us. This is as large as what the late turn gains. What sets it stays open.
- A product of 128x1024 on GpSimd, 2.4 us, can hold a VectorE CAST, scalar operation or subtraction for about as long: 0.43 became 2.57 us, and the price in T = 14 was 13.5 us for work that nobody waited for.
- Passes into different quarters start 7 ns apart, though the records have 109 ns from start to end for a load of 32 columns and 222 for a matmul. In grouped, passes of the next quarter even start ahead of the last ones of the quarter before.
